# The last products of a LayerNorm: two fused instructions on VectorE in place of three on GpSimd, in 47 batches

## Chip, cores, metric
One core of one Trainium2 chip. The time is that of the whole kernel on the device, in microseconds (us), the median over runs.

## The reference
An adaLN block over x of shape (8, 512, 128). First a causal attention with its LayerNorm and gates, then a stack of six layers, each with a windowed (local) attention and a feed-forward part. Cut to the feed-forward part of one of the six layers, which is where the change lies:

```python
def ffn_layer(x, g, bln, W1, b1, W2, b2):
    mu = x.mean(-1, keepdims=True)
    var = ((x - mu) ** 2).mean(-1, keepdims=True)
    xn = (x - mu) / jnp.sqrt(var + 1e-05) * g + bln
    hg = xn @ W1 + b1
    a, gate = jnp.split(hg, 2, -1)
    return a * jax.nn.gelu(gate, approximate=False) @ W2 + b2
for i in range(DEPTH):          # DEPTH = 6
    x = attn_layer(shift_tokens(x), Wqkv[i], q_scale[i], k_scale[i], Wo[i]) + x
    x = ffn_layer(shift_tokens(x), ln_g[i], ln_b[i], W1[i], b1[i], W2[i], b2[i]) + x
```

## The kernel before
The causal attention of the 8 batch elements takes the first 650 us or so. Then come 6 layers x 8 elements = 48 local batches, v = 0 to 47, `final` = 47. Every engine works through a written list of steps (TENSOR, SCALAR, VECTOR, GPSIMD, SYNC), repeated for each batch, in which a step's suffix says how many batches ahead it belongs. The engines run their own list in order, and meet through one semaphore per kind of step (`done(kind, ...)`). So a step that is late holds up all that stands behind it in its engine's list, and steps of several batches are under way at once. The PSUM halves A, B (psA in the profile) and C, D (psB) go from step to step: a step on TensorE waits until the last reader of its bank has ended (`take`, LAST). Products in 16 bits are made of a high and a low part; steps that end in h make the high part on ScalarE, those that end in l the low part on VectorE or GpSimd.

The LayerNorm of a batch, centred values on 128 partitions x 512 tokens:
- la (TensorE): x minus its mean, into psA. lq (ScalarE L1094): its square, into f_a. lw (ScalarE L1099): a copy, into f_c. lb (TensorE): the mean of the squares, v, into psB (bank C).
- lr (ScalarE L1106, L1108, L1110): f_r = Exp(-0.5 Ln(v + 1e-5)), then f_a = f_r squared / 2.
- ln (VectorE L1397): f_a = (v + 1e-5) f_a. In the first batch of a layer five small instructions for the biases (L1393 to L1396) stand before it.
- lx: one Newton step, f_c = (1.5 - f_a) (f_r f_c). In batches 0 to 46 it is GpSimd's: L1504 (1.5 - f_a), L1506 (f_r f_c), L1508 (their product). In the final batch VectorE does it with two instructions of two operations each: L1386, ahead of ln, makes f_c = -f_r f_c, and L1402 f_c = (f_a - 1.5) f_c.
- fh (ScalarE L1128): the high part of f_c. fl (GpSimd L1511): its low part; in the last layer fl also adds to the kept output. f (TensorE): the product with W1.

What stands around ln and lx in the lists:
- VectorE: tc13, ts13 (L1339, L1349: the rotary products h and ts of a projection in psB), ln, ol00 (L1330: low part of an attention output in psA), sm10 (L1368, L1370: sums of the softmax and their reciprocals), mx11 (L1361: negated maxima, negm), tc00, ts00. In five batches, one for each change of layer, a weight's low part (wl01, L1282) stands ahead of ln, and another (wl10) behind it.
- GpSimd: ad12 (L1476, L1477: h -+ ts), gl2, gl1 (L1523), lx, nw1 (L1484, L1486, L1488: the same Newton step for q and k), pn10 (L1501: the softmax's quotients pb), cs1 (L1491), fl, ct1 (L1496: n_b, for TensorE's step bc), xl, ad.
- ScalarE: ex, fh, oe, ca1 (L1057: n_c, which cs1 takes), ve, cb1.
- TensorE: ss1, sc110, tp01 (L760: transposes, into bank C, which ln must have freed), three more sc, pj00 (the projection psA<-xs, into bank B, which ol00 must have freed), pv010, ng11 (psA<-negm, with the maxima of mx11). bc10 and bc11 (psA, psB<-n_b) come later.

The lists become each engine's walk in `program`, with the final batch's steps put apart:

```python
last_vector = [("ln", final), ("lx", final), ("fl", final), ("fr", final - 1), ("fm", final, 2), ("fm", final, 0),
               ("gl", final, 2), ("fm", final, 1), ("gl", final, 0), ("gl", final, 1), ("fr", final)]
vector_walk = [s for s in vector_walk if s not in last_vector] + last_vector
gpsimd_walk = [s for s in gpsimd_walk if s not in last_vector]
```

Of the kernel before, what the change touches and what calls it, by code (L numbers as in the profile page):

```python
# [218 lines left out]
def program(nc, xt, wqa, wka, wva, wo, wqk, wvl, wof, w1, w2, vecs, scl, ct, wmod, tab, masks, left, mats, out):  # L219
    ctx, early = ExitStack(), ExitStack()  # L220
    with ctx:
# [112 lines left out]
                       ("gl", final, 2), ("fm", final, 1), ("gl", final, 0), ("gl", final, 1), ("fr", final)]  # L334
        scalar_walk = [s for s in scalar_walk if s not in last_scalar] + last_scalar
        vector_walk = [s for s in vector_walk if s not in last_vector] + last_vector
        gpsimd_walk = [s for s in gpsimd_walk if s not in last_vector]
        homes[("op", final)] = "Al"
        homes[("f", final, 1)] = "C"
        count = ordinals((gpsimd_walk, tensor_walk, scalar_walk, vector_walk, sync_walk))  # L340
# [944 lines left out]
        def local_vector(e):  # L1285
            for n in range(2):
                e.wait_ge(s_xk[n], 4)
            for s in vector_walk[3:]:
# [52 lines left out]
                elif kind == "ts":  # L1341
                    c = s[2]
                    i = count[s] - 1
                    if i >= 2:
                        e.wait_ge(*done("ad", *ts_walk[i - 2][1:]))
                    if v // 2 % NB == 0:
                        e.wait_ge(*done("tb", v // 2, c % 2 * 2 + 1))
                    e.wait_ge(*done("sq", v, c))
                    e.tensor_tensor(flat(tsb[i % 2]), psum(("pj", v, c))[:, :], flat(t_rot[:, c % 2, 1, :, :]), ALU.mult  # L1349
                                    ).then_inc(ended["ts"])  # L1350
                elif kind == "bm":
                    c = s[2]
                    h = halves(made(v, c))
                    r = psum(("bc", v, c // 2))[:, 512 * (c % 2):512 * (c % 2) + 512].rearrange("p (a n) -> p a n", a=2)
                    e.wait_ge(*done("bc", v, c // 2))
                    e.wait_ge(*done("ad", v, c))
                    e.tensor_tensor(h, h, r.unsqueeze(1).to_broadcast([128, 2, 2, S // 2]), ALU.mult).then_inc(ended["bm"])  # L1357
                elif kind == "mx":
                    rp = s[2]
                    e.wait_ge(*all_done("sc", *((v, rp, t) for t in range(NT))))  # L1360
                    e.tensor_reduce(negm[rp][:, :], psum(("sc", v, rp, 0)).rearrange("p (a s) -> p a s", a=16), AXX, ALU.max,  # L1361
                                    negate=True).then_inc(ended["mx"])
                elif kind == "sm":
                    rp = s[2]
                    if v:
                        e.wait_ge(*done("pn", v - 1, rp))
                    e.wait_ge(*done("ex", v, rp))
                    e.tensor_reduce(sums[rp][:, :], pbs[rp].rearrange("p x t (f s) -> p (x t f) s", f=2), AXX, ALU.add).then_inc(s_rc)  # L1368
                    e.wait_ge(s_rc, count[s])
                    e.reciprocal(rc[rp][:, :], sums[rp][:, :]).then_inc(ended["sm"])  # L1370
                elif kind == "rs":
                    b = v % NB
                    o = psum(("op", v))
                    e.wait_ge(*done("op", v))
                    e.scalar_tensor_tensor(out=xb[0:64, b, 0:S], in0=o[0:64, 0:512], scalar=1.0 / WS, in1=xb[0:64, b, 0:S],
                                           op0=ALU.mult, op1=ALU.add)
                    e.scalar_tensor_tensor(out=xb[64:128, b, 1:S + 1], in0=o[64:128, 0:512], scalar=1.0 / WS,
                                           in1=xb[64:128, b, 1:S + 1], op0=ALU.mult, op1=ALU.add).then_inc(ended["rs"])
                elif kind == "ln":
                    li = v // NB  # L1380
                    o = psum(("lb", v))
                    vl = V_LAYER + 10 * li
                    if v == final:
                        e.wait_ge(s_lrr, v + 1)
                        e.wait_ge(*done("lw", v))
                        e.scalar_tensor_tensor(out=f_c[:, :], in0=f_r[:, :], scalar=-1.0, in1=f_c[:, :], op0=ALU.mult,  # L1386
                                               op1=ALU.mult).then_inc(s_neg)
                    e.wait_ge(*done("lr", v))
                    if v % NB == 0:
                        if v:  # L1390
                            e.wait_ge(*all_done("ge", *((v - 1, j) for j in range(3))))
                        for j in range(3):
                            e.tensor_scalar(b1s[0:FP[j], j:j + 1], o[0:FP[j], 512 + j:513 + j],  # L1393
                                            t_vec[0:FP[j], vl + 4 + j:vl + 5 + j], WF, ALU.add, ALU.mult)
                        e.tensor_tensor(b1s[:, 3:5], o[:, 515:517], t_vec[:, vl + 7:vl + 9], ALU.add)
                        e.tensor_tensor(b1s[0:FP[2], 5:6], o[0:FP[2], 517:518], t_vec[0:FP[2], vl + 9:vl + 10], ALU.add)  # L1396
                    e.scalar_tensor_tensor(out=f_a[:, :], in0=o[:, 0:512], scalar=1e-5, in1=f_a[:, :], op0=ALU.add,  # L1397
                                           op1=ALU.mult).then_inc(ended["ln"])
                elif kind == "lx":
                    e.wait_ge(s_neg, 1)  # L1400
                    e.wait_ge(*done("ln", v))
                    e.scalar_tensor_tensor(out=f_c[:, :], in0=f_a[:, :], scalar=-1.5, in1=f_c[:, :], op0=ALU.add, op1=ALU.mult  # L1402
                                           ).then_inc(ended["lx"])
                elif kind == "fl":
                    b = v % NB
                    e.wait_ge(*done("fh", v))
                    e.tensor_tensor(f_cl[:, :], f_c[:, :], f_ch[:, :], ALU.subtract).then_inc(ended["fl"])
                    e.wait_ge(s_x1d[b], 32)
                    e.wait_ge(s_z, b + 1)
                    e.tensor_tensor(kept[b], kept[b], f_x[:, :], ALU.add).then_inc(s_y)  # L1410
                elif kind == "fm":
                    j = s[2]
                    n = FP[j]
                    if v == final:
                        e.wait_ge(*done("f", v, j))
                    e.wait_ge(*done("ge", v, j))
                    e.scalar_tensor_tensor(out=f_g[j][0:n, :], in0=psum(("f", v, j))[0:n, 0:512], scalar=b1s[0:n, j:j + 1],
                                           in1=f_g[j][0:n, :], op0=ALU.add, op1=ALU.mult).then_inc(ended["fm"])
                elif kind == "gl":
                    j = s[2]  # L1420
                    n = FP[j]
                    e.wait_ge(*done("gh", v, j))
                    e.tensor_tensor(f_gl[j][0:n, :], f_g[j][0:n, :], f_gh[j][0:n, :], ALU.subtract).then_inc(ended["gl"])
                elif kind == "fr":
                    b, li = v % NB, v // NB
                    o = psum(("fo", v))
                    if li == L - 1:
                        y = kept[b]
                        e.wait_ge(s_y, b + 1)
                        e.wait_ge(*done("fo", v))  # L1430
                        e.scalar_tensor_tensor(out=y, in0=o[:, 0:512], scalar=t_gz[:, b:b + 1], in1=y, op0=ALU.mult, op1=ALU.add
                                               ).then_inc(ended["fr"])
                        continue
                    e.wait_ge(*done("fo", v))
                    e.scalar_tensor_tensor(out=xb[0:64, b, 0:S], in0=o[0:64, 0:512], scalar=1.0 / WF / WF,
                                           in1=xb[0:64, b, 0:S], op0=ALU.mult, op1=ALU.add)
                    e.scalar_tensor_tensor(out=xb[64:128, b, 1:S + 1], in0=o[64:128, 0:512], scalar=1.0 / WF / WF,
                                           in1=xb[64:128, b, 1:S + 1], op0=ALU.mult, op1=ALU.add).then_inc(ended["fr"])
# [24 lines left out]
        def local_gpsimd(e, steps):  # L1463
            for s in steps:
# [32 lines left out]
                elif kind == "pn":  # L1497
# [1 line left out]
                    w = pbs[rp].rearrange("p x t (f s) -> p (x t f) s", f=2)  # L1499
                    e.wait_ge(*done("sm", v, rp))  # L1500
                    e.tensor_tensor(w, w, rc[rp][:, :].unsqueeze(2).to_broadcast([128, 16, 2 * W]), ALU.mult).then_inc(ended["pn"])  # L1501
                elif kind == "lx":
                    e.wait_ge(*done("ln", v))
                    e.tensor_scalar(f_a[:, :], f_a[:, :], -1.0, 1.5, ALU.mult, ALU.add).then_inc(s_lxh)  # L1504
                    e.wait_ge(*done("lw", v))
                    e.tensor_tensor(f_c[:, :], f_r[:, :], f_c[:, :], ALU.mult).then_inc(s_lxh)  # L1506
                    e.wait_ge(s_lxh, 2 * (v + 1))
                    e.tensor_tensor(f_c[:, :], f_a[:, :], f_c[:, :], ALU.mult).then_inc(ended["lx"])  # L1508
                elif kind == "fl":
                    e.wait_ge(*done("fh", v))  # L1510
                    e.tensor_tensor(f_cl[:, :], f_c[:, :], f_ch[:, :], ALU.subtract).then_inc(ended["fl"])  # L1511
# [71 lines left out]
```

## Time and profile before

| | |
|---|---|
| median of 3 runs | 3506.13 us (3495.59 to 3508.76) |
| the profiled execution, time | 3492.28 us |
| its span | 3490.5 us |
| TensorE (PE) busy | 3310.8 us, 95% of the span |
| GpSimd (POOL) busy | 2900.1 us, 83% |
| VectorE (DVE) busy | 2950.8 us, 85% |
| ScalarE (ACT) busy | 2468.1 us, 71% |
| mean granted clock of TensorE | 0.989 |

Busy times are of the one profiled execution. PE is the matmul, PEld its weight load, which overlaps it; a matmul's end is modelled, so a busy PE is not one at its peak. Shares over the whole span mix the causal part, where GpSimd is half idle, with the 48 local batches; the stretch from 800 to 3400 us is local batches alone.

### The profile page before, as it was taken

The page shows a single profiled execution, that of the slowest core. Times are in us where ns is not written, and L with a number is a line of the kernel's source. Part 1 is how long each engine was busy: PE and PEld are TensorE (multiplying, and loading weights), DVE is VectorE, ACT ScalarE, POOL GpSimd, SP SyncE. Part 2 cuts the span into 40 slices and gives each one's busy share as a digit, 9 for nine tenths or more (in the row PEclk, how much of TensorE's full clock was granted, in tenths as well). Part 3 has the DMA queues.
Part 4 walks back from the last instruction along what each step waited for, and adds up shares of the span by engine and source line. Part 5 has one row for each costly group of instructions (what it writes and reads, how often), then busy time and mean ns, then how long its engine had stood idle before and what let it go on. Part 6 is the DMA issues. An engine that isn't in the chain of part 4 may idle for free.

```text
span 3490.5 us, 158023 instructions
## 1 busy us (share of the span) xinstructions
PE 3310.8 (95%) x69988; PEld 1939.0 (56%) x69988; DVE 2950.8 (85%) x3108; ACT 2468.1 (71%) x3349; POOL 2900.1 (83%) x2478
## 2 busy tenths in 40 slices
PE   7999999679999999999999999999999999999997
PEld 4666666445555555555555555555555555555554
DVE  7888888578888988888888889888898888988884
ACT  5777777556777767777767677677776777767774
POOL 3655555588999989998989999899999999989993
PEclk9999999889999999999999999999999999999998
DMA  1000000154545555545455545455454645555543
GB/s 67 5 5 5 5 5 7 42 119 102 142 111 126 121 116 125 135 106 131 106 133 117 123 114 125 111 134 125 109 131 102 144 114 132 127 127 117 125 109 79
DMA packets 163861, 347.33 MB, mean 100 GB/s; under 512 B 32876, under 2 KB 42352, under 8 KB 153840
## 3 DMA queue, kind: packets, MB, share of 16 engines
q1 hardware_dynamic: 163184, 337.23, 40.9%
q8 instruction: 556, 9.11, 1.2%
q14 instruction: 121, 0.99, 0.1%
HBM read 24.62 MB, written 4.19 MB: 8 GB/s over the span
## 4 chain that ended last, share of the span: by engine, by line
PE 71%; DVE 12%; issue 5%; POOL 5%; ACT 4%; SPq 1%; DMA 1%; DVEq 0%; POOLq 0%; ACTq 0%
PE psA L703 30%; PE psB L703 23%; PE psB L565 7%; PE psA L565 6%; PE psB L760 3%; DVE h L1357 3%; DVE pt L1256 1%; PE psA L760 1%; SPq L496 1%; DVE negm L1361 1%; DVE sum L1368 1%; DVE ts L1349 1%; POOL sq L1481 1%; DVE h L1339 1%; POOL h L1477 1%
## 5 line engine op out<-in xcount | busy, mean ns | idle before, releaser
L1448 POOL TENSOR_TENSOR pt<-wk,pt 128x256 f16<-128x256 f32 (+3 forms) x256 | 368.0, 1453 | 285.0 <-ACT pt L950 195.3
L1481 POOL TENSOR_TENSOR sq<-sq 128x512 f32<-128x512 f32 x384 | 487.4, 1277 | 81.5 <-ACT sq L1040 80.6
L1476 POOL TENSOR_TENSOR h<-h,ts 128x512 f32<-128x512 f32 x384 | 498.4, 1298 | 1.2 <-DVE ts L1349 1.2
L1477 POOL TENSOR_TENSOR h<-h,ts 128x512 f32<-128x512 f32 x384 | 495.1, 1289 | 0.0
L1357 DVE TENSOR_TENSOR h<-h,psB 128x1024 f32<-128x1024 f32 x288 | 337.9, 1215 | 56.7 <-PE psB L703 55.1
L1501 POOL TENSOR_TENSOR pb<-pb,rc 128x1024 f32<-128x1024 f32 x192 | 365.4, 1903 | 9.8 <-DVE rc L1370 9.4
L1339 DVE TENSOR_TENSOR h<-psA,t_rot 128x1024 f32<-128x1024 f32 x192 | 234.3, 1220 | 72.1 <-ACT sq L1040 64.9
L703 PE MATMUL psA<-kf,qf 64*32 64x64 f32 x18432 | 256.8, 224 | 24.8 <-issue 24.2
L703 PEld LDWEIGHTS psA<-kf,qf 64*32 64x32 f32 x18432 | 194.6, 106 | 131.6 <-issue 130.9
L1339 DVE TENSOR_TENSOR h<-psB,t_rot 128x1024 f32<-128x1024 f32 x192 | 233.6, 1217 | 28.9 <-ACT sq L1040 21.5
L1040 ACT ACTIVATE sq<-psA 128x1024 f32<-128x1024 f32 x192 | 197.0, 1027 | 67.5 <-PE psA L703 67.3
L1040 ACT ACTIVATE sq<-psB 128x1024 f32<-128x1024 f32 x192 | 196.0, 1021 | 59.1 <-PE psB L703 55.6
L1368 DVE TENSOR_REDUCE sum<-pb 128x16 f32<-128x1024 f32 x192 | 232.4, 1211 | 3.9 <-ACT pb L1073 3.5
L1349 DVE TENSOR_TENSOR ts<-psB,t_rot 128x1024 f32<-128x1024 f32 x192 | 233.0, 1214 | 1.8 <-POOL h L1477 1.8
L1349 DVE TENSOR_TENSOR ts<-psA,t_rot 128x1024 f32<-128x1024 f32 x192 | 230.6, 1201 | 0.0
L1073 ACT ACTIVATE pb<-psA 128x1024 f32<-128x1024 f32 x144 | 146.8, 1019 | 105.2 <-PE psA L703 104.9
L703 PEld LDWEIGHTS psA<-ptb,vev 64*64 64x64 f32 x6144 | 167.1, 135 | 97.1 <-issue 66.7
L703 PE MATMUL psB<-ptb,vev 64*64 64x32 f32 x6144 | 199.7, 222 | 12.7 <-issue 9.6
L703 PEld LDWEIGHTS psB<-ptb,vev 64*64 64x64 f32 x6144 | 168.9, 135 | 75.2 <-issue 52.2
L703 PE MATMUL psB<-ptb,vo 64*64 64x32 f32 x6144 | 198.5, 220 | 8.5 <-issue 8.4
L703 PE MATMUL psA<-ptb,vev 64*64 64x32 f32 x6144 | 201.3, 222 | 3.7 <-issue 2.1
L1361 DVE TENSOR_REDUCE negm<-psA 128x16 bf16<-128x1024 f32 x144 | 175.4, 1218 | 34.7 <-PE psA L703 32.7
(372 smaller groups left out, 10244.0 us busy)
## 6 DMA issues: line engine op xcount, KB each, us to landing
qf<-h SPq DMA_DIRECT2D x768, 136.0 KB, 2.5
kf<-h SPq DMA_DIRECT2D x768, 136.0 KB, 2.5
vev<-vo SPq DMA_DIRECT2D x288, 256.0 KB, 4.0
vev<-vo SPq DMA_DIRECT2D x96, 192.0 KB, 4.6
stage<-wqk SPq DMA_DIRECT2D x24, 256.0 KB, 4.9
stage<-wvl SPq DMA_DIRECT2D x12, 256.0 KB, 4.9
stage<-wof SPq DMA_DIRECT2D x12, 256.0 KB, 5.4
xb<-xt SPq DMA_DIRECT2D x8, 256.0 KB, 7.8
```

Of the source, the lines that this page charges most:

```text
L565: return e.matmul(o, l, r, start=start, stop=stop, skip_group_check=True, **kw)
L703: return e.matmul(o, l, r, start=start, stop=stop, skip_group_check=True, **kw)
L1040: e.activation(flat(sqb[c]), psum(("pj", v, c))[:, :], ACT.Square).then_inc(ended["sq"])
L1339: e.tensor_tensor(halves(made(v, c)), by_halves(psum(("pj", v, c))[:, :]), by_halves(flat(t_rot[:, c % 2, 0, :, :])), ALU.mult).then_inc(e ...
L1349: e.tensor_tensor(flat(tsb[i % 2]), psum(("pj", v, c))[:, :], flat(t_rot[:, c % 2, 1, :, :]), ALU.mult).then_inc(ended["ts"])
L1357: e.tensor_tensor(h, h, r.unsqueeze(1).to_broadcast([128, 2, 2, S // 2]), ALU.mult).then_inc(ended["bm"])
L1368: e.tensor_reduce(sums[rp][:, :], pbs[rp].rearrange("p x t (f s) -> p (x t f) s", f=2), AXX, ALU.add).then_inc(s_rc)
L1448: e.tensor_tensor(pt[g][pr][:, :, 1, o:o + w], wk[(slot_of(s)[0] - 1) % SLOTS][:, :, 0:w], pt[g][pr][:, :, 0, o:o + w], ALU.subtract).then ...
L1476: e.tensor_tensor(halves_of(h, 0), halves_of(h, 0), t[1], ALU.subtract)
L1477: e.tensor_tensor(halves_of(h, 1), halves_of(h, 1), t[0], ALU.add).then_inc(ended["ad"])
L1481: e.tensor_tensor(sqb[c][:, 0, :], sqb[c][:, 0, :], sqb[c][:, 1, :], ALU.add).then_inc(ended["qa"])
L1501: e.tensor_tensor(w, w, rc[rp][:, :].unsqueeze(2).to_broadcast([128, 16, 2 * W]), ALU.mult).then_inc(ended["pn"])
```

## The change
In batches 0 to 46 lx goes from GpSimd's list to VectorE's, right behind ln; the product that stood ahead of ln in the final batch alone now stands there in all; lx waits for that product's semaphore with the batch's count.

```diff
-        gpsimd_walk = [s for s in gpsimd_walk if s not in last_vector]
+        vector_walk = [t for s in vector_walk for t in ((s, ("lx", s[1])) if s[0] == "ln" and s[1] < final else (s,))]
+        gpsimd_walk = [s for s in gpsimd_walk if s not in last_vector and s[0] != "lx"]
...
                     vl = V_LAYER + 10 * li
-                    if v == final:
-                        e.wait_ge(s_lrr, v + 1)
-                        e.wait_ge(*done("lw", v))
-                        e.scalar_tensor_tensor(out=f_c[:, :], in0=f_r[:, :], scalar=-1.0, in1=f_c[:, :], op0=ALU.mult,
-                                               op1=ALU.mult).then_inc(s_neg)
+                    e.wait_ge(s_lrr, v + 1)
+                    e.wait_ge(*done("lw", v))
+                    e.scalar_tensor_tensor(out=f_c[:, :], in0=f_r[:, :], scalar=-1.0, in1=f_c[:, :], op0=ALU.mult,
+                                           op1=ALU.mult).then_inc(s_neg)
                     e.wait_ge(*done("lr", v))
...
                 elif kind == "lx":
-                    e.wait_ge(s_neg, 1)
+                    e.wait_ge(s_neg, v + 1)
                     e.wait_ge(*done("ln", v))
                     e.scalar_tensor_tensor(out=f_c[:, :], in0=f_a[:, :], scalar=-1.5, in1=f_c[:, :], op0=ALU.add, op1=ALU.mult
                                            ).then_inc(ended["lx"])
...
-                elif kind == "lx":
-                    e.wait_ge(*done("ln", v))
-                    e.tensor_scalar(f_a[:, :], f_a[:, :], -1.0, 1.5, ALU.mult, ALU.add).then_inc(s_lxh)
-                    e.wait_ge(*done("lw", v))
-                    e.tensor_tensor(f_c[:, :], f_r[:, :], f_c[:, :], ALU.mult).then_inc(s_lxh)
-                    e.wait_ge(s_lxh, 2 * (v + 1))
-                    e.tensor_tensor(f_c[:, :], f_a[:, :], f_c[:, :], ALU.mult).then_inc(ended["lx"])
```

On VectorE, around ln of batch 34, before and then with the change:

```order
L1339 TENSOR_TENSOR h<-psB,t_rot 128x2x2x256
L1349 TENSOR_TENSOR ts<-psB,t_rot 128x1024
L1397 SCALAR_TENSOR_TENSOR f_a<-psB,f_a 128x512
L1330 TENSOR_TENSOR otl<-psA,oth 128x1024
L1368 TENSOR_REDUCE sum<-pb 128x16
L1370 RECIPROCAL rc<-sum 128x16
L1361 TENSOR_REDUCE negm<-psA 128x16
```

```order
L1340 TENSOR_TENSOR h<-psB,t_rot 128x2x2x256
L1350 TENSOR_TENSOR ts<-psB,t_rot 128x1024
L1386 SCALAR_TENSOR_TENSOR f_c<-f_r,f_c 128x512
L1397 SCALAR_TENSOR_TENSOR f_a<-psB,f_a 128x512
L1402 SCALAR_TENSOR_TENSOR f_c<-f_a,f_c 128x512
L1331 TENSOR_TENSOR otl<-psA,oth 128x1024
L1369 TENSOR_REDUCE sum<-pb 128x16
L1371 RECIPROCAL rc<-sum 128x16
L1362 TENSOR_REDUCE negm<-psA 128x16
```

L1386 and L1402 have come in on both sides of ln, ahead of ol, sm and mx; the line numbers after them shift by one because of the diff.

On GpSimd, at the same batch, before and then with the change:

```order
L1477 TENSOR_TENSOR h<-h,ts 128x2x256
L1523 TENSOR_TENSOR f_gl<-f_g,f_gh 85x512
L1523 TENSOR_TENSOR f_gl<-f_g,f_gh 128x512
L1504 TENSOR_SCALAR f_a<-f_a 128x512
L1506 TENSOR_TENSOR f_c<-f_r,f_c 128x512
L1508 TENSOR_TENSOR f_c<-f_a,f_c 128x512
L1484 TENSOR_TENSOR n_a<-n_s,n_a 128x256
L1486 TENSOR_SCALAR n_a<-n_a 128x256
L1488 TENSOR_TENSOR n_a<-n_a,n_r 128x256
L1501 TENSOR_TENSOR pb<-pb,rc 128x1024
L1491 TENSOR_TENSOR n_a<-n_a,n_c 128x256
```

```order
L1477 TENSOR_TENSOR h<-h,ts 128x2x256
L1516 TENSOR_TENSOR f_gl<-f_g,f_gh 85x512
L1516 TENSOR_TENSOR f_gl<-f_g,f_gh 128x512
L1484 TENSOR_TENSOR n_a<-n_s,n_a 128x256
L1486 TENSOR_SCALAR n_a<-n_a 128x256
L1488 TENSOR_TENSOR n_a<-n_a,n_r 128x256
L1501 TENSOR_TENSOR pb<-pb,rc 128x1024
L1491 TENSOR_TENSOR n_a<-n_a,n_c 128x256
```

The three instructions of lx are gone, and nw follows gl. TensorE's and ScalarE's lists are as before.

## Rows read from the trace of the kernel before

**Rows 1.** Busy time by stretch: stretch, its length, busy time (instructions) of each engine, clock, DMA
```profile
800.00:3400.00 2600.00, 2519.94 (x57257) 1444.24 (x57255) 2258.38 (x2295) 1880.62 (x2504) 2401.00 (x2098) 1.00 0.52 121
```
**Rows 2.** The old lx, by line: count, ns min/median/max, first and last start in us
```profile
L1504 POOL TENSOR_SCALAR f_a<-f_a x47: 607/616/649, 807.4 to 3433.3; 128x512 f32<-128x512 f32 x47
...
L1506 POOL TENSOR_TENSOR f_c<-f_r,f_c x47: 1252/1267/1297, 808.0 to 3433.8; 128x512 f32<-128x512 f32 x47
...
L1508 POOL TENSOR_TENSOR f_c<-f_a,f_c x47: 1262/1268/1753, 809.3 to 3435.2; 128x512 f32<-128x512 f32 x47
```
**Rows 3.** Waits from 800 to 3400 us: who waits for whom, us in total, times, longest
```profile
PEld psB L703 <- DVE h L1357: 45.1, 91, 0.9
PEld psA L703 <- DVE ts L1349: 40.2, 82, 0.8
...
DVE b1s L1393 <- ACT f_a L1110: 3.6, 6, 0.7
...
PE psA L703 <- POOL n_b L1496: 2.4, 6, 0.7
```
**Rows 4.** The chain of waits, in mid-period: start in us, us, what
```profile
1935.00 1.28 DVE h L1357 x2
```
**Rows 5.** VectorE's instructions with two SBUF inputs, by line: as rows 2
```profile
L1386 DVE SCALAR_TENSOR_TENSOR f_c<-f_r,f_c x1: 692/692/692, 3474.4 to 3474.4; 128x512 f32<-128x512 f32 x1
...
L1402 DVE SCALAR_TENSOR_TENSOR f_c<-f_a,f_c x1: 691/691/691, 3475.9 to 3475.9; 128x512 f32<-128x512 f32 x1
...
L1282 DVE SCALAR_TENSOR_TENSOR wql<-stage,wqh x24: 675/871/1886, 661.0 to 2986.7; 128x512 f16<-128x512 f32 x24
```
**Rows 6.** VectorE: ln by line with its idle time, then batch 34 in order
```profile
L1397 DVE SCALAR_TENSOR_TENSOR f_a<-psB,f_a x48: 674/680/693, 806.6 to 3475.1; 128x512 f32<-128x512 f32 x48
...
  ACT f_a L1110: 1.9, 1
...
2750.81 0.68 DVE L1397 SCALAR_TENSOR_TENSOR f_a<-psB,f_a 128x512 f32<-128x512 f32 x1
2752.19 1.23 DVE L1330 TENSOR_TENSOR otl<-psA,oth 128x1024 f16<-128x1024 f32 x1 [0.69 <-ACT oth L1088]
...
2755.01 1.23 DVE L1361 TENSOR_REDUCE negm<-psA 128x16 bf16<-128x1024 f32 x1 [0.18 <-PE psA L703]
2757.53 1.23 DVE L1339 TENSOR_TENSOR h<-psA,t_rot 128x1024 f32<-128x1024 f32 x1 [1.29 <-ACT sq L1040]
```
**Rows 7.** A weight split on VectorE and what runs beside it on GpSimd, in order
```profile
2916.97 0.73 DVE L1282 SCALAR_TENSOR_TENSOR wql<-stage,wqh 128x512 f16<-128x512 f32 x1
...
2917.12 1.72 POOL L1477 TENSOR_TENSOR h<-h,ts 128x512 f32<-128x512 f32 x1
```
**Rows 8.** GpSimd in batch 34, in order
```profile
2749.60 1.28 POOL L1476 TENSOR_TENSOR h<-h,ts 128x512 f32<-128x512 f32 x1
2750.84 1.27 POOL L1477 TENSOR_TENSOR h<-h,ts 128x512 f32<-128x512 f32 x1
...
2761.34 0.67 POOL L1491 TENSOR_TENSOR n_a<-n_a,n_c 128x256 f32<-128x256 f32 x1
```
**Rows 9.** TensorE in batch 34, in order, then ln and the transposes of batch 37
```profile
2752.78 1.09 PE L760 MATMUL psB<-t_mats,pb 128*128 128x128 f32 x8
...
2754.90 0.39 PE L703 MATMUL psA<-xs0h,wql 128*128 128x512 f16 x1
...
2757.37 0.60 PE L703 MATMUL psA<-negm,t_masks 128*128 128x512 bf16 x2
...
2917.63 0.68 DVE L1397 SCALAR_TENSOR_TENSOR f_a<-psB,f_a 128x512 f32<-128x512 f32 x1
...
2919.01 1.09 PE L760 MATMUL psB<-t_mats,pb 128*128 128x128 f32 x8
```
**Rows 10.** ScalarE in batch 34: n_c
```profile
2760.42 0.51 ACT L1057 ACTIVATE n_c<-n_a,t_mats 128x256 bf16<-128x256 f32 x1
```
**Rows 11.** TensorE in the last layer: a wait for n_b
```profile
3276.94 0.39 PE L703 MATMUL psA<-n_b,t_masks 32*128 32x256 bf16 x4 [0.72 <-POOL n_b L1496]
```

## The prediction, made before the change had run

> **What bounds the kernel now.** I read the local batches only, since the change touches nothing before them. First the busy time by stretch [rows 1]: from 800 to 3400 us TensorE is busy 2519.94 of 2600 us (97%), GpSimd 2401.00 (92%), VectorE 2258.38 (87%), and the granted clock is at its upper level (2.4 GHz). So TensorE has little to lose and little to win. The period of a batch comes from GpSimd's first instruction of the old step: 47 times between 807.4 and 3433.3 us [rows 2], so (3433.3 - 807.4) / 46 = 57.1 us. Per period that makes TensorE busy 55.3, GpSimd 52.7 and VectorE 49.6 us. Next the waits [rows 3]. The reader is to see who holds TensorE: its weight loads stand 45.1 us for VectorE's products on h and 40.2 us for its ts products, about 0.5 us each time, while its matmuls waited for GpSimd's n_b 6 times, 2.4 us in all. Then the chain of waits [rows 4]: in the middle of a period it runs through VectorE (the products on h at 1935.00), which TensorE had released. VectorE waits there for TensorE first, so what it is late at ln is gone by then. What counts is the ten microseconds after ln.
>
> **What is removed.** 47 times GpSimd drops one instruction of 0.61 us and two of 1.27 [rows 2]: 3.15 us, 148 us in all.
>
> **What is added.** 47 times VectorE takes two instructions, the product of f_r and f_c ahead of ln and lx behind it. The final batch has both already: 692 and 691 ns [rows 5]. With lx's wait on ln (which costs the overlap of two neighbours, about 0.1 us) that is 0.6 + 0.6 + 0.2 = 1.4 us of VectorE's queue. The new first wait is for the Exp and the copy of ScalarE. It costs nothing: ln itself waits for a later instruction of ScalarE and stood idle for it once, 1.9 us [rows 6]; in the six batches that open a layer VectorE waits 3.6 us in all there [rows 3], and the new product fills that gap.
>
> **The price hidden in these two.** Both read two tensors from SBUF. The nearest rows are the weight splits, also f32 pairs from SBUF: they take 675 ns at least, 871 as a median and 1886 at most [rows 5]. One of them shows why [rows 7]: the split at 2916.97 lasts 0.73 us, and GpSimd's instruction that starts under it takes 1.72 instead of 1.27. In the other order the split waits until GpSimd's running instruction ends. The Trainium skill, "SBUF — State Buffer", section "Who interferes with whom", says the same of a VectorE instruction with two SBUF inputs beside a GpSimd one that reads SBUF, in words that speak against this change; the trace agrees in both directions, 0.45 us on one side and up to 1.2 on the other. So GpSimd does not win 3.15 us but 3.15 - 2 x 0.45 = 2.2, and on VectorE the addition lies between 1.4 us (GpSimd between instructions) and 2 x 1.2 more, 3.8 us.
>
> **A typical batch, step by step** (batch 34, ln at 2750.81 [rows 6]). GpSimd is 1.21 us into an instruction of 1.28 [rows 8]: 0.07 left. The new product starts at 2750.81, waits that, ends near 2751.56. ln runs to 2752.2. GpSimd's next instruction (2750.84) is held up and ends near 2752.6 in place of 2752.1; lx, ready at 2752.3, waits for it and ends near 2753.25. So the queue moves on 1.8 us later than now (2751.4). Now who is behind it:
> - The transposes of the other half on TensorE take the bank that ln frees: they start at 2752.78 [rows 9]; ln ends at 2752.2. Nothing lost.
> - ol starts at 2752.19 now because it waits for ScalarE [rows 6]; then at 2753.2, ending 2754.4. The projection that takes its bank starts at 2754.90 [rows 9]. Nothing lost.
> - sm and mx follow without a gap: mx, now at 2755.01, ends at 2757.0 instead of 2756.24. TensorE's step on negm starts at 2757.37 [rows 9]. Nothing lost, 0.4 us left.
> - tc has 1.29 us of idle time in front, waiting for ScalarE [rows 6]. There the delay ends.
>
> I went through all 46 starts of ln from batch 0 to 45 in the same way, with GpSimd's instruction of that moment. In 26 batches GpSimd has under 0.3 us left at that moment, six open a layer, one has 0.6 us left with room behind it: 0. In eight batches over 1.1 us is left, and ln ends 1.2 us later than above; the tightest shows it [rows 9]: ln at 2917.63 and the transposes at 2919.01, so 1.3 us lost. Worked through, the eight lose 7 us (one has no loss, one 0.05). In the five batches that have a weight split behind ln (they are among the 26) about 0.5 us each, 2.5 us. In five batches of the last layer 0.65 us is left: 0.2 each, 1 us. Together +10.5 us on TensorE's path, which I cut to 9.5 as some of it falls where TensorE waits for VectorE anyway.
>
> **What GpSimd's time is worth.** In most batches nothing: after lx it runs into its next wait, cs on ScalarE's n_c. In the typical batch n_c ends at 2760.93 [rows 10] and cs starts at 2761.34 [rows 8]: 0.4 us can be had of the 2.2, and no one is waiting for it. f_c comes 5 us earlier, but ScalarE takes it in its own order. In the last layer GpSimd has one more product per batch, and TensorE does wait for n_b: 0.72 us in the longest case [rows 11]. Those waits go: -3 us, counting two in mid-period.
>
> Sum: +9.5 - 3 = +6.5 us against the profiled execution's 3492.28 us, 3498.8. That execution lies 13.85 us under the median of the runs shown, 3506.13, so the median becomes 3512.6, rounded **3513 us**. A measurement of this kernel tells about 0.5% (17.5 us) from nothing, and this is inside.
>
> **The rivals.**
> 1. The locks fall in TensorE's path in every batch (slower). Mechanism: GpSimd's place at ln shifts, since it has lost 2.2 us of work, and each new instruction finds a whole one of 1.27 us before it. Place: ln, the transposes behind it, ol. It decides once over some 0.6 us are left at ln: the transposes have 0.6 us of room in the typical batch. Price: about 1.1 us in 46 batches, +50, 3556 us. For it: the eight batches above, and the 1886 ns. Against it: GpSimd waits for ScalarE and TensorE ten microseconds before ln, so its place there is fixed by them. Chance 0.18. Half of that effect (+18 to +30) 0.05.
> 2. GpSimd is the hidden bound (faster). In 17 of 47 batches it has no idle time before cs, and the shortest periods are among these. If all of the 2.2 us came through there, -37 us, 3469. Against it: 2.4 us of waiting of TensorE for GpSimd [rows 3], and the 0.4 us above. Chance 0.12.
> 3. The new instructions run at half rate. By the rows it is excluded (691 ns for 512 elements, ln with one input from PSUM takes 680 [rows 5, 6]); if it were so, VectorE would be 1.1 us later in each batch, 0.7 beyond the room of 0.4, 46 times: +32 us, 3545. Chance 0.02. The Trainium skill, "Vector Engine (DVE) Microarchitecture Reference", section "Points that are easy to get wrong", states such halving for a scalar_tensor_tensor with two non-bf16 SBUF sources; the final batch's rows disagree.
> 4. The change does nothing at all, as the losses don't come and only the n_b waits go: -3 us, 3503. Chance 0.06.
>
> The forecast itself has 0.57. Slower by over 0.5%: 0.18 + 0.05 + 0.02 = 0.25. Faster: 0.12. Within: 0.63. The range reaches from 3476 (most of the way to rival 2) to 3552 (the near half of rival 1).
>
> **What would show it.** Right: 48 instances of each new line with medians between 0.7 and 1.0 us and maxima near 1.9; ol's idle time before it nearly gone; GpSimd's busy time down by about 100 us, its idle time before cs up by 1 to 2 us a batch; the n_b waits of the last layer gone; the transposes behind ln late in few batches. Wrong: VectorE's f_a as a releaser of TensorE with over 20 us in the waits (rival 1); a period under 56.5 us (rival 2); new lines of over 1.2 us at least (rival 3).

## The result and the profile after

The median with the change is 3512.98 us (3504.42 to 3522.47, 20 runs), that of the kernel before, run in turn with it, 3504.6 us (3495.59 to 3514.04, 20 runs). The ratio is 1.0028 with a 95% interval of 1.002 to 1.0036: slower by 0.28%, 9.8 us of 3504.6, with 7.0 to 12.6 us as the interval. The two medians by themselves differ by 8.4 us. The forecast was +6.5 us and 3513.

First the stretch of local batches alone, the same as [rows 1] (stretch, length, busy time and instructions of TensorE, its weight loads, VectorE, ScalarE, GpSimd, then clock and DMA):

```profile
800.00:3400.00 2600.00, 2510.65 (x57019) 1437.60 (x57007) 2336.75 (x2377) 1871.13 (x2495) 2285.15 (x1951) 1.00 0.52 121
```

GpSimd has gone from 2401.00 to 2285.15 us, VectorE from 2258.38 to 2336.75, and the clock is the same at two digits. TensorE's busy time is 9.3 us shorter in the same 2600 us, and it did 238 matmuls fewer, 0.4% (the stretch cuts the batches at other points than before, and some matmul records can be missing): that is the loss. Now the waits in that stretch (who waits for whom: us in total, times, longest), beside [rows 3]:

```profile
POOL n_a L1491 <- ACT n_c L1058: 154.9, 91, 5.6
...
DVE otl L1331 <- ACT oth L1089: 39.7, 51, 1.7
```

In the same view of the kernel before, the first stood at 51.8 us and the second at 75.5. So 103 of the 116 us that GpSimd saved were turned into waiting for ScalarE's n_c, and VectorE's delay is seen in ol, which has less to wait for. TensorE alone, first before (n_b into psA is in [rows 3]), then after:

```profile
PE psA L703 <- DVE ts L1349: 2.3, 6, 0.4
PE psB L703 <- POOL n_b L1496: 1.4, 2, 1.0
...
PE psA L703 <- DMA kf<-h: 1.1, 5, 0.3
...
PE psB L703 <- DVE ts L1349: 0.7, 1, 0.7
PE psB L703 <- DVE otl L1330: 0.6, 1, 0.6
...
PE psB L760 <- DVE f_a L1397: 0.5, 1, 0.5
```

```profile
PE psB L761 <- DVE f_a L1397: 5.9, 5, 2.6
PE psA L704 <- DVE ts L1350: 4.0, 9, 0.7
PE psA L704 <- DVE otl L1331: 2.4, 5, 1.1
PE psA L704 <- DMA kf<-h: 2.1, 6, 0.7
PE psB L704 <- POOL n_b L1496: 1.7, 4, 0.7
PE psA L704 <- POOL n_b L1496: 1.4, 5, 0.5
...
PE psB L704 <- DVE otl L1331: 0.6, 1, 0.6
```

Subtract line by line: the transposes waiting for ln (f_a) +5.4, the projection waiting for ol (otl) 3.0 - 0.6 = +2.4, ts 4.0 - 3.0 = +1.0, the DMA of kf +1.0, n_b 3.1 - 3.8 = -0.7. Together +9.1 us, beside 9.3 us less of busy time. That this is also within 0.7 us of the measured 9.8 is partly chance: these are two single executions, which differ by 12.0 us in span (3490.5 and 3502.5), and the times of one kernel spread over 18 us. Last the two new lines and ln between them (count, ns min/median/max, first and last start):

```profile
L1386 DVE SCALAR_TENSOR_TENSOR f_c<-f_r,f_c x48: 681/774/4114, 803.9 to 3486.4; 128x512 f32<-128x512 f32 x48
...
L1397 DVE SCALAR_TENSOR_TENSOR f_a<-psB,f_a x48: 673/678/692, 805.1 to 3487.1; 128x512 f32<-128x512 f32 x48
...
L1402 DVE SCALAR_TENSOR_TENSOR f_c<-f_a,f_c x48: 692/982/1652, 805.9 to 3487.9; 128x512 f32<-128x512 f32 x48
```

ln has one input in PSUM and keeps its length, 673 to 692 ns; its two neighbours, with both inputs in SBUF, do not. The step by step of the forecast can be read in batch 34, VectorE and then GpSimd:

```profile
2759.17 0.68 DVE L1386 SCALAR_TENSOR_TENSOR f_c<-f_r,f_c 128x512 f32<-128x512 f32 x1
2759.77 0.69 DVE L1397 SCALAR_TENSOR_TENSOR f_a<-psB,f_a 128x512 f32<-128x512 f32 x1
2760.56 0.98 DVE L1402 SCALAR_TENSOR_TENSOR f_c<-f_a,f_c 128x512 f32<-128x512 f32 x1
2761.46 1.21 DVE L1331 TENSOR_TENSOR otl<-psA,oth 128x1024 f16<-128x1024 f32 x1
...
2764.00 1.16 DVE L1362 TENSOR_REDUCE negm<-psA 128x16 bf16<-128x1024 f32 x1
2766.21 1.23 DVE L1340 TENSOR_TENSOR h<-psA,t_rot 128x1024 f32<-128x1024 f32 x1 [1.05 <-ACT sq L1041]
```

```profile
2757.96 1.28 POOL L1476 TENSOR_TENSOR h<-h,ts 128x512 f32<-128x512 f32 x1
2759.21 1.78 POOL L1477 TENSOR_TENSOR h<-h,ts 128x512 f32<-128x512 f32 x1
2760.95 2.73 POOL L1516 TENSOR_TENSOR f_gl<-f_g,f_gh 85x512 f16<-85x512 f32 x2
...
2770.01 0.67 POOL L1491 TENSOR_TENSOR n_a<-n_a,n_c 128x256 f32<-128x256 f32 x1 [2.48 <-ACT n_c L1058]
```

From the start of the new product, where ln used to start, ol comes 2761.46 - 2759.17 = 2.29 us later; before it was 1.38 [rows 6], and 2.4 was forecast. mx ends after 5.99 us; 6.2 was forecast. tc still has 1.05 us of idle time in front of it, so the delay ends there. On the other side GpSimd's L1477 under the product takes 1.78 us in place of 1.27 [rows 8], lx waits until it ends (2760.99) and takes 0.98, and cs then waits 2.48 us for n_c.

### The profile page after: what moved, and what is told of

It reads as the page before. It is cut to its first block, busy times and chain, and to the rows that moved or that the text cites. A ratio compares the mean times of both kernels' runs of the same rounds, so it can differ in the third digit from the quotient of the medians.

```text
span 3502.5 us, 158070 instructions
## 1 busy us (share of the span) xinstructions
PE 3311.8 (95%) x69988; PEld 1939.3 (55%) x69988; DVE 3040.6 (87%) x3202; ACT 2466.6 (70%) x3349; POOL 2793.3 (80%) x2337
## 4 chain that ended last, share of the span: by engine, by line
PE 68%; DVE 14%; issue 7%; POOL 5%; ACT 4%; SPq 1%; DMA 1%; DVEq 0%; POOLq 0%; ACTq 0%
PE psA L704 28%; PE psB L704 22%; PE psB L566 7%; PE psA L566 6%; DVE h L1358 3%; PE psB L761 3%; DVE ts L1350 2%; DVE h L1340 2%; DVE pt L1257 1%; PE psA L761 1%; DVE sum L1369 1%; DVE negm L1362 1%; SPq L497 1%; POOL sq L1481 1%; POOL h L1477 1%
## 5 line engine op out<-in xcount | busy, mean ns | idle before, releaser
L1477 POOL TENSOR_TENSOR h<-h,ts 128x512 f32<-128x512 f32 x384 | 512.9, 1336 | 0.0
L1476 POOL TENSOR_TENSOR h<-h,ts 128x512 f32<-128x512 f32 x384 | 497.2, 1295 | 1.2 <-DVE ts L1350 1.2
L1516 POOL TENSOR_TENSOR f_gl<-f_g,f_gh 128x512 f16<-128x512 f32 x141 | 192.0, 1374 | 19.2 <-ACT f_gh L1138 19.2
L704 PE MATMUL psA<-ptb,vo 64*64 64x32 f32 x6144 | 199.7, 220 | 6.5 <-issue 6.3
```

Of the source, the lines that this page charges most:

```text
L704: return e.matmul(o, l, r, start=start, stop=stop, skip_group_check=True, **kw)
L1476: e.tensor_tensor(halves_of(h, 0), halves_of(h, 0), t[1], ALU.subtract)
L1477: e.tensor_tensor(halves_of(h, 1), halves_of(h, 1), t[0], ALU.add).then_inc(ended["ad"])
```

## The experiments

The question was what of the loss is queue time on VectorE and what comes of the two new instructions meeting GpSimd's, and whether GpSimd's freed time is worth anything. Every ratio is to the kernel before on the same chip, with its 95% interval. Sizes of single waits come from one profile each.

**1. GpSimd's relief alone.** lx is left out in batches 0 to 46: GpSimd loses its three instructions and VectorE gets none. f (the product with W1) then reads ScalarE's copy of the centred values times 0.05, so the last products of the second norm are not computed; waits on lx go to ln.

```diff
-        gpsimd_walk = [s for s in gpsimd_walk if s not in last_vector]
+        gpsimd_walk = [s for s in gpsimd_walk if s not in last_vector and s[0] != "lx"]
...
+            if kind == "lx" and at[0] < final:
+                kind = "ln"
...
-                    e.activation(f_c[:, :], psum(("la", v))[:, 0:512], ACT.Copy).then_inc(ended["lw"])
+                    e.activation(f_c[:, :], psum(("la", v))[:, 0:512], ACT.Copy, scale=0.05).then_inc(ended["lw"])
```

> Leaves lx out in batches 0 to 46: GpSimd drops its three instructions, nothing comes to VectorE, f_c is an unnormalised copy. What GpSimd's 3.15 us a batch are worth by themselves. Theory (GpSimd hides behind the others): 0 to -5 us against before, since TensorE waited for n_b 2.4 to 3.8 us in all. Rival (GpSimd is the hidden bound, and the two new instructions ate its gain): -20 us or more, a period of 56.6 us or less.

Measured: 3491.86 us against 3492.99, ratio 0.9998 (0.9986 to 1.0011). The hidden bound of the second rival would have been 0.9894. The wait list says where the time went:

```profile
POOL n_a L1493 <- ACT n_c L1059: 157.9, 91, 4.0
```

This is the change's 154.9 again. The expectation (0 to -5 us) was met. With VectorE's list as it is, unloading GpSimd at this place wins no more than the lower end of the interval, 5 us.

**2. and 3. Two extra instructions on VectorE, GpSimd unchanged.** The kernel before gets two instructions per batch at the places of the new ones, once with one SBUF input (a reduction of 450 elements) and once with two (a product of 450 elements into a scratch tensor).

```diff
+                    else:
+                        e.wait_ge(s_lrr, v + 1)
+                        e.tensor_reduce(t_dm[:, 0:1], t_mats[:, 0:450], AXX, ALU.max)
...
+                    if v < final:
+                        e.wait_ge(*done("ln", v))
+                        e.tensor_reduce(t_dm[:, 1:2], t_mats[:, 0:450], AXX, ALU.max)
```

In the other kernel each reduction is replaced by this:

```diff
+                        e.scalar_tensor_tensor(out=t_dm[:, 0, :], in0=t_mats[:, 0:450], scalar=-1.0, in1=t_mats[:, 0:450],
+                                               op0=ALU.mult, op1=ALU.mult)
```

> Before, plus two reductions of 450 constant elements in SBUF on VectorE in 47 batches, one ahead of ln (waiting for the Exp), one behind ln (waiting for ln): the queue time of the change without two SBUF inputs. Theory (the lock costs): 0 to +3 us against before. Rival (VectorE's time itself costs): +8 us or more, like the change.

> The same with two scalar_tensor_tensor of two SBUF inputs each, 450 elements, in the same places, results unused; GpSimd keeps its lx. Theory: each lasts 0.6 us to 1.9 us, one ahead of ln longer at times, +8 to +15 us against before, and over 5 us more than the reductions; TensorE waits for f_a as with the change. Rival (VectorE's time itself): the same as with the reductions within 3 us.

Measured: without a second input 3504.51 us, ratio 1.0034 (1.002 to 1.0048); with it 3507.45, ratio 1.0035 (1.0021 to 1.0049). The reductions took 0.61 and 0.62 us, the products 0.88 and 1.06 as means. Both are about +12 us by the ratio. The theory of the locks wanted 0 to +3 us for the first, and over 5 us between the two; it got neither, and the rival's numbers (+8 us or more, and the two within 3 us) came in both times. The profile of the first shows one reason. VectorE, then GpSimd, then TensorE:

```profile
2524.82 0.62 DVE L1405 TENSOR_REDUCE t_dm<-t_mats 128x1 f32<-128x450 f32 x1
2525.36 4.23 DVE L1283 SCALAR_TENSOR_TENSOR wql<-stage,wqh 128x512 f16<-128x512 f32 x1
2529.51 1.21 DVE L1331 TENSOR_TENSOR otl<-psA,oth 128x1024 f16<-128x1024 f32 x1
```

```profile
2524.94 2.28 POOL L1530 TENSOR_TENSOR f_gl<-f_g,f_gh 85x512 f16<-85x512 f32 x2
2527.19 0.62 POOL L1511 TENSOR_SCALAR f_a<-f_a 128x512 f32<-128x512 f32 x1
2527.78 1.26 POOL L1513 TENSOR_TENSOR f_c<-f_r,f_c 128x512 f32<-128x512 f32 x1
2529.12 1.59 POOL L1515 TENSOR_TENSOR f_c<-f_a,f_c 128x512 f32<-128x512 f32 x1
```

```profile
2530.78 0.39 PE L704 MATMUL psA<-xs0h,wql 128*128 128x512 f16 x1 [3.16 <-DVE otl L1331]
```

The reductions keep their length (608 to 624 ns), but they push the weight split, which has two SBUF inputs, under a train of GpSimd instructions. It takes 4.23 us; its longest in the kernel before is 1886 ns [rows 5]. Three of the five splits behind ln did so (4.14, 4.23 and 4.14 us), and TensorE's waits for ol behind them were 1.17, 3.16 and 2.73 us, 7.1 in all where the kernel before has 0.6. So this kernel was not the test without locks that it was meant to be, and the train is longer here because GpSimd still has its own lx in it. These waits account for 6.5 of the 12 us; the rest is open. In the profile of the second kernel the longest split took 1.83 us, and TensorE waited 3.7 us for f_a, 4.9 for ol and 7.7 for n_b, where the kernel before has 0.5, 0.6 and 3.8. Experiments 9 and 10 make the comparison again with GpSimd's list of the change.

**4. ln first.** The change, with the product moved behind ln, so that the transposes get their bank 0.6 us or more earlier.

```diff
-                    e.wait_ge(s_lrr, v + 1)
-                    e.wait_ge(*done("lw", v))
-                    e.scalar_tensor_tensor(out=f_c[:, :], in0=f_r[:, :], scalar=-1.0, in1=f_c[:, :], op0=ALU.mult,
-                                           op1=ALU.mult).then_inc(s_neg)
+                    if v == final:
...
+                    if v < final:
+                        e.wait_ge(*done("lw", v))
+                        e.scalar_tensor_tensor(out=f_c[:, :], in0=f_r[:, :], scalar=-1.0, in1=f_c[:, :], op0=ALU.mult,
+                                               op1=ALU.mult).then_inc(s_neg)
```

> The change, with the product of f_r and f_c behind ln in batches 0 to 46: VectorE's order is ln, product, lx. Theory: ln ends as early as before, TensorE's waits for f_a (5.9 us in the change) go, those for otl stay or grow by 1 to 3 us; +3 to +6 us against before instead of +9. Rival (the place does not matter, the total on VectorE or GpSimd's shifted timing does): +8 to +11 us as with the change.

Measured: 3512.72 us, ratio 1.0058 (1.0043 to 1.0072), +20 us; missed, and above the rival's +8 to +11 too. The waits for f_a are gone, and in their place:

```profile
PE psA L704 <- DVE otl L1331: 20.7, 30, 2.4
```

The same two instructions on the same data now take 1.40 us each as a mean, 1.06 and 1.00 in the change, and in this order they start 0.6 us later against GpSimd's instructions. TensorE waits for ol 30 times. The change itself cost +8 to +14 us in its three measurements (the result, experiments 8 and 11), so the order costs 6 to 12 us more. It differs in little but the longer instructions and where they start; which of the two carries how much was not separated.

**5. Both behind mx.** The two instructions stand behind mx11, where the forecast's step by step left VectorE idle ahead of tc.

```diff
-        vector_walk = [t for s in vector_walk for t in ((s, ("lx", s[1])) if s[0] == "ln" and s[1] < final else (s,))]
+        late, held = [], []
+        for s in vector_walk:
+            late.append(s)
+            if s[0] == "ln" and s[1] < final:
+                held.append(("lx", s[1]))
+            if held and (s[0] == "mx" and s[2] == 1):
+                late += held
+                held = []
+        vector_walk = late + held
...
```

The product goes into lx, as in experiment 4.

> The change with both instructions moved in VectorE's queue from around ln to behind mx11, where 1.29 us of idle time stood in front of tc. Theory (what costs is that ln, ol and mx end late, not the total on VectorE): TensorE's waits for f_a and otl go back to those of before (0.5 and 0.6 us), 0 to +4 us against before. Rival (VectorE's total time, 90% busy, is what costs wherever it stands): +8 us or more.

Measured: 3515.53 us against 3479.89, ratio 1.0109 (1.0089 to 1.0129), +38 us; missed by far, and within what the rival forecast (+8 us or more). The waits for f_a did go; the loss stands in another place:

```profile
PE psA L712 <- DVE ts L1358: 39.2, 41, 1.5
```

```profile
L1415 DVE SCALAR_TENSOR_TENSOR f_c<-f_a,f_c x48: 691/2274/2278, 812.6 to 3495.8; 128x512 f32<-128x512 f32 x48
```

The idle time before tc was real, but lx there meets GpSimd's long product of the softmax (1.89 to 1.93 us in the kernel before) and takes 2.27, and a step of TensorE waits 41 times for ts behind it. No run puts two reductions in this place, so how much of the 38 us is the longer lx and how much is plain queue time, as the rival has it, is not shown.

**6. Half of it, ahead of ln.** Only the product f_r f_c is VectorE's; GpSimd keeps f_a - 1.5 and the last product, and lx stays in its list.

```diff
+                    e.tensor_scalar(f_a[:, :], f_a[:, :], -1.5, None, ALU.add).then_inc(s_lxh)
+                    e.wait_ge(s_neg, v + 1)
+                    e.wait_ge(s_lxh, v + 1)
+                    e.tensor_tensor(f_c[:, :], f_a[:, :], f_c[:, :], ALU.mult).then_inc(ended["lx"])
```

> Half of the change: the product of f_r and f_c on VectorE ahead of ln, the other two operations stay on GpSimd (f_a - 1.5 and one product). Theory: VectorE's queue is 0.7 us late instead of 1.8, the waits for f_a stay (about 6 us, some long ones), those for otl go: +3 to +8 us against before. Rival (the instruction behind ln is what costs): 0 to +2 us.

Measured: 3483.0 us, ratio 1.0016 (1.0004 to 1.0028), +5.6 us: as expected. TensorE waited 6.1 us for f_a, six times, and 8.3 us for n_b where it was 3.8 before; no wait for ol stands in that view. GpSimd was busy 2412.94 us of the stretch from 800 to 3400, 2401.00 before [rows 1], although it has a product less. The reason is in f_a - 1.5, which is written with one operation here and took 0.62 us with its two operations before [rows 2]:

```profile
L1503 POOL TENSOR_SCALAR f_a<-f_a x47: 1479/1485/1862, 807.2 to 3421.4; 128x512 f32<-128x512 f32 x47
```

So this version does not relieve GpSimd, and its +5.6 us is not the price of the product on VectorE alone. The same split with the two-operation form was not tried.

**7. The other half, behind mx.** GpSimd makes the product f_r f_c in lx's old place, ScalarE's copy carries the sign, and VectorE does lx alone behind mx11 (the list as in 5); no product stands ahead of ln except in the final batch.

```diff
+        gpsimd_walk = [("fp", s[1]) if s[0] == "lx" else s for s in gpsimd_walk if s not in last_vector]
...
+                    e.activation(f_c[:, :], psum(("la", v))[:, 0:512], ACT.Copy, scale=-1.0).then_inc(ended["lw"])
...
+                elif kind == "fp":
+                    e.wait_ge(*done("lr", v))
+                    e.wait_ge(*done("lw", v))
+                    e.tensor_tensor(f_c[:, :], f_r[:, :], f_c[:, :], ALU.mult).then_inc(s_neg)
```

> A candidate: GpSimd makes the product of f_r and f_c where lx stood (one instruction of 1.27 us for three), ScalarE's copy of lw carries the minus sign, VectorE has one instruction alone, behind mx11. Theory: at most 0.7 us in an idle gap of 1.29 us, GpSimd's 1.4 us of gain worth nothing: -2 to +3 us against before. Rival (total on VectorE): +3 us or more.

Measured: 3485.34 us, ratio 1.0014 (0.9995 to 1.0032). The interval holds no change as well as +11 us; it tells only that this is no gain of more than 2 us. The median, +5 us, lies outside the expected -2 to +3 and fits the rival. TensorE waited 11.5 us for ol and 4.8 for ln, and all of it stands behind five weight splits, at four of the five changes of layer. The longest, one that stands ahead of ln, and TensorE's wait behind it:

```profile
2910.95 6.02 DVE L1291 SCALAR_TENSOR_TENSOR wql<-stage,wqh 128x512 f16<-128x512 f32 x1
```

```profile
2917.63 1.97 PE L769 MATMUL psB<-t_mats,pb 128*128 128x128 f32 x8 [4.76 <-DVE f_a L1405]
```

The other four, behind ln, took 5.49 to 5.60 us, with waits for ol of 2.78 to 2.94. That is 16.3 us of waiting in this profile, the slowest of the kernel's 12 runs. Whether this version would win with the splits in another place was not tried.

**8. The change again, beside 5 to 7.**

> The change once more, on the same chip as the three beside it: +7 to +13 us against before. If it falls outside, the comparison between chips is what varies, not the place of the instructions.

Measured: 3492.51 us, ratio 1.0041 (1.0023 to 1.0059). The ratio makes it +14 us, just above the +13 expected; the medians differ by 12.6. The new lines took 0.99 and 1.03 us; TensorE waited 3.8 us for f_a, 2.9 for ol, 5.5 for ts.

**9. and 10. Relief, with the queue time alone and with the locks.** Both are experiment 1, so GpSimd has the change's list and its freed time, plus the two extra instructions of experiments 2 and 3 on VectorE. The pair differs in the second SBUF input, and in that the product writes 450 elements and the reduction one. ln also writes its whole result, 512 elements, and with one input in PSUM keeps its length. The queue time is 0.61 + 0.62 = 1.23 us, where the change's own is 1.4 at least.

> GpSimd's list is that of the change (its three instructions of lx are gone; f_c is ScalarE's copy times 0.05, so the LayerNorm's last products are left out), and VectorE has two reductions of 450 elements (one SBUF input, about 0.61 us) in the places of the two new instructions: the change's queue time without its locks. If the locks make the cost (theory of the prediction: 1.4 us of queue has room, the waits of 0.6 to 1.2 us beside GpSimd do not), the ratio is 0.999 to 1.001, so 0 to +4 us, the reductions last 0.61 to 0.63 us each with no long one, and TensorE waits under 1 us for f_a. If queue time alone makes it (rival), the ratio is 1.002 to 1.004, as the change's.

> As relief_no_lock, but with two instructions of two SBUF inputs of the same 450 elements in a scratch tensor. Theory of the locks: instances from 0.61 up to 2 us or more, median 0.8 to 1.0, ratio 1.002 to 1.004, at least 5 us more than relief_no_lock. Rival (queue time alone): within 2 us of relief_no_lock.

Measured, against 3484.66 us: without locks 3485.55 us, ratio 1.0001 (0.9988 to 1.0014); with locks 3491.57, ratio 1.0021 (1.0008 to 1.0034). Both ratios are as expected. The 12 runs of the one and the 12 of the other compared directly: the medians differ by 6.0 us, the means by 6.8, with 3 to 10 us as the 95% interval. The instructions without and with a second input:

```profile
L1393 DVE TENSOR_REDUCE t_dm<-t_mats x47: 608/610/622, 803.5 to 3419.5; 128x1 f32<-128x450 f32 x47
```

```profile
L1393 DVE SCALAR_TENSOR_TENSOR t_dm<-t_mats x47: 616/703/1816, 807.3 to 3431.0; 128x450 bf16<-128x450 f32 x47
...
L1408 DVE SCALAR_TENSOR_TENSOR t_dm<-t_mats x47: 627/987/1656, 809.2 to 3432.4; 128x450 bf16<-128x450 f32 x47
```

And TensorE's waits, without and with:

```profile
PE psA L706 <- DVE ts L1352: 4.0, 9, 0.6
PE psA L706 <- DVE otl L1333: 2.9, 3, 1.4
```

```profile
PE psA L706 <- DVE ts L1352: 5.3, 11, 0.7
PE psB L763 <- DVE f_a L1404: 4.7, 6, 1.4
PE psA L706 <- DVE otl L1333: 4.5, 4, 2.1
```

The waits for f_a are there only with the second input. The longest instances are 1.8 us and the medians 0.70 and 0.99, a little under what was expected (2 us, and 0.8 to 1.0). The splits are not free of the reductions here either: three of them take 2.37 to 2.49 us, and the waits for ol (2.9 us) are right behind those. The Trainium skill, "SBUF — State Buffer", section "Who interferes with whom", says that a reduction never contends with GpSimd on this chip, and that an instruction with two SBUF inputs contends with a GpSimd instruction that reads SBUF; the 608 to 622 ns of the 47 reductions ahead of ln beside up to 1816 agree.

**11. The change once more, beside 9 and 10.**

> The change itself on this chip, as the yardstick for the other two: ratio 1.002 to 1.005; new instructions mean 1.0 us.

Measured: 3493.12 us, ratio 1.0022 (1.0007 to 1.0037), as expected, and the same as with the scratch instructions that lock (1.0021). The means of the new instructions were 1.15 and 1.01 us. TensorE waited 9.8 us for f_a and 4.3 for ol; the product's longest was here 4.27 us.

No version of the eleven was measurably faster than the kernel before.

Experiments 2 and 9 put the same two reductions on VectorE and differ in GpSimd's list alone: 1.0034 (from 1.002) with GpSimd's lx still there, 1.0001 (up to 1.0014) without it. So GpSimd's freed time, worth nothing by itself in experiment 1, is worth about 11 us once VectorE carries two more instructions. The long splits are the part of it that the profiles show (4.14 to 4.23 us against 2.37 to 2.49).

## Why the prediction was right

- **The number.** The measured 3512.98 beside the forecast 3513 is luck. The kernel before measured 1.5 us lower than the forecast's base (3504.6 for 3506.13), and the change added 8.4 us by the medians in place of 6.5. The +6.5 lies just under the interval of the difference, 7.0 to 12.6. Its terms missed in both directions, as below.
- **GpSimd's time is worth nothing.** Right for an unchanged VectorE, and shown by experiment 1. 103 of its 116 us went into the wait of cs for n_c, where the forecast had put them. The second rival (-37 us) is excluded by the interval. Experiments 2 and 9 show what the forecast did not have: with more work on VectorE the shorter GpSimd list is worth some 11 us.
- **VectorE's queue has room for the instructions themselves.** Right. The typical batch came out as worked through (2.29 us for 2.4, 5.99 for 6.2), and experiment 9 gives the queue time a price of +0.3 us, within -4 to +5. That holds for 1.23 us of queue time with GpSimd's shorter list; with the list of before it does not (experiment 2).
- **The locks are the price.** Right in direction, and shown by experiments 9 to 11: 1.0001 without and 1.0021 with, the same as the change's 1.0022 beside them. The two ratios' intervals overlap (up to 1.0014 and from 1.0008), since each also carries the scatter of the kernel before; compared directly the two differ by 3 to 10 us, and the waits for f_a are absent without a second input. Experiment 4 fits it: longer meetings with GpSimd go with 6 to 12 us more. Experiments 2 and 3 did not tell the two apart with GpSimd unchanged. The first was spoilt at least in part by the pushed weight splits; how much of their 12 us is locks and how much queue time stays open.
- **The eight batches with over 1.1 us left, 7 us.** The size was near, the form was not. TensorE waited for f_a in five batches, +5.4 us, of which 2.6 in one. The forecast's bound for one instruction was 1.2 us of waiting. That failed in batch 11, where the product took 4.11 us (see below); the others were 0.4 to 1.1. The tightest batch of the forecast, 37, was hit, with 1.02 us of waiting for the forecast's 1.3 (its own rows give nearer 1.2: 2917.63 + 1.39 + 1.2 - 2919.01). The other seven are not named, so whether the right batches were hit can't be told.
- **Five batches with a weight split, 2.5 us.** Near in size, again with another form. TensorE's wait for ol rose by 2.4 us, but of the waits only three, 1.7 us, stand behind splits; two more, 0.7 us, do not. In the same three batches TensorE then waits for ts, 0.72, 0.61 and 0.32 us, for which the forecast had no term.
- **The last layer's 1 us** was not seen: its waits for ts are six of 0.37 to 0.39 us before and six of 0.38 or 0.39 after. The waits for the DMA of kf rose by 1.0, which had no term either. The cut from 10.5 to 9.5 is shown by no run.
- **The n_b waits, -3 us.** This term was too large. They fell from 3.8 to 3.1 us in the trace, in the last layer from 2.4 to 1.4 (up to 3400 us), and did not go. ct waits for ScalarE's n_c 45 times in the stretch, 31.1 us both before and after, so there GpSimd's earlier work did not set when it started. It is the step "those waits go", and it makes 2.3 of the 3.3 us between +9.8 and +6.5.
- **Rivals.** The first (locks in every batch, +50) would have shown over 20 us of waits for f_a: 5.9, 3.8 and 9.8 in three profiles. Something of its kind exists in other orders: experiment 4 has 30 waits at ol, and experiment 5 has 41 at ts. Half rate is excluded by the shortest of 681 and 692 ns.
- **The signs.** The medians of the new lines (0.77 and 0.98 us) and GpSimd's busy time (116 us less) came as said. The maxima did not (4.11 us for 1.9), ol's idle time halved (75.5 to 39.7 us) and did not nearly go, cs waited 2.3 us a batch more for 1 to 2, and the n_b waits of the last layer stayed.

## What to carry to other kernels

Before moving work to an engine with idle time, look for what the relieved engine will wait for next: if that is a third engine, the relief wins nothing by itself. It can still pay for part of what the move costs, here some 11 us (experiments 2 and 9). An instruction of VectorE with two SBUF inputs has to be costed by what GpSimd runs beside it at that moment, here 0.68 us alone, about 1.0 as a mean, and up to 4.3; a weight split, pushed to another place among GpSimd's instructions, took up to 6.0. With one input in PSUM, or as a reduction, it kept its length. An idle gap in an engine's timeline is no room for an instruction until one has looked at who waits behind the gap and which neighbour stands beside it.

## What was not expected of the hardware

A waiting VectorE instruction with two SBUF inputs can be passed over by more than one GpSimd instruction. In batch 11 of the change, VectorE, GpSimd and TensorE:

```profile
1432.49 4.11 DVE L1386 SCALAR_TENSOR_TENSOR f_c<-f_r,f_c 128x512 f32<-128x512 f32 x1
1436.53 0.68 DVE L1397 SCALAR_TENSOR_TENSOR f_a<-psB,f_a 128x512 f32<-128x512 f32 x1
```

```profile
1431.30 1.28 POOL L1476 TENSOR_TENSOR h<-h,ts 128x512 f32<-128x512 f32 x1
1432.54 1.29 POOL L1477 TENSOR_TENSOR h<-h,ts 128x512 f32<-128x512 f32 x1
1433.77 2.28 POOL L1516 TENSOR_TENSOR f_gl<-f_g,f_gh 85x512 f16<-85x512 f32 x2
1436.59 0.72 POOL L1484 TENSOR_TENSOR n_a<-n_s,n_a 128x256 f32<-128x256 f32 x1 [0.54 <-ACT n_a L1055]
```

```profile
1437.26 1.97 PE L761 MATMUL psB<-t_mats,pb 128*128 128x128 f32 x8 [2.56 <-DVE f_a L1397]
```

```profile
1437.00:1441.00 4.00, 3.74 (x105) 3.08 (x106) 3.60 (x6) 1.03 (x1) 2.28 (x4) 0.50 0.02 4
```

GpSimd ran L1477 and both instructions of L1516 at their full speed while the product stood, then went idle at 1436.05, and the product ended 0.55 us later, at 1436.60. In batch 34 the same pair in the same order, at almost the same distance (0.04 us instead of 0.05 between the two starts), went the other way: the product took 0.68 us and L1477 was held up to 1.78. The same long product came twice in the profile of experiment 11 (4.25 and 4.27 us) and once in that of experiment 6 (4.28). Weight splits did it three times in that of experiment 2 (4.14 to 4.23) and five times in that of experiment 7 (5.49 to 6.02). Experiment 4 has 3.68 us for its product and 3.74 for a split, experiment 5 3.72 for a split. In experiment 8 there was none, and its ratio was not lower for it. So it is rare for the product, and in experiment 7 it came at four of the five changes of layer. It has cost TensorE up to 4.76 us at a time, and what decides it was not found.

The last row above (the fields are those of [rows 1]) shows a second cost. Behind the wait of 2.56 us the granted clock was 0.50, its lower level (1.2 GHz), from 1437 to 1441 us, and the eight transposes took 1.97 us, where they take 1.09 in [rows 9]. From 800 to 3400 us the clock fell three times in the profile before and three times with the change; this fall lasted twice as long as the others, which makes some 1.7 us. It does not follow every such wait: behind the 3.16 us of experiment 2 the next matmul took 0.39 us, as in [rows 9].
